# One query product a step earlier, value and probability products of self attention a step later, in a two-attention and experts kernel

## The chip, the cores and the metric

The kernel runs on one core of one Trainium2 chip. The metric is the device time of one execution, in microseconds, as the median of several runs. All times below that are not medians come from one profiled execution of the same program.

## The reference, cut to what matters

One layer with three residual parts over x of 32 batches, 32 positions and 256 features:

```python
x = x + xattn(layernorm(x), ctx_512, ...)   # 16 heads, 257 context rows of 64 features, rotary context
x = x + attn(layernorm(x), ...)             # self attention over the 32 positions of a batch, 16 heads of 128
x = x + ffn(layernorm(x), ...)              # router, 8 of 64 experts, capacity 128, silu gate

# self attention
q = x @ (wq_codes * repeat(wq_scales, 32)) + bq     # k and v in the same way
scores = einsum('bqhd,bkhd->bhqk', q, k) / sqrt(128)
out = einsum('bhqk,bkhd->bqhd', softmax(scores), v)
return out @ (wo_codes * repeat(wo_scales, 32)) + bo

# cross attention, after folding its weights
scores = einsum('bhsr,bhlr->bhsl', q_r, k_r)        # 257 keys a batch
ctx_c = einsum('bhsl,bld->bhsd', softmax(scores), kv_rope)
```

## The kernel before, in words

The 1024 rows of x are eight tiles of 128 rows, each holding four batches. A software pipeline of three stages runs over them: while tile i is in cross attention, tile i-1 is in self attention and tile i-2 in the output product of self attention and the router. Before the pipeline stands a part that folds and dequantises weights, behind it one that runs the 64 experts and adds their rows up. The change touches the pipeline alone.

A pipeline tile is 21 steps, written out by hand and the same on every engine. In step r (0 to 15) TensorE makes the scores of one row of cross attention (`score_row`, lines 1189 and 1190), VectorE takes the row's maximum (line 830), ScalarE the exponential (line 609). Two steps later TensorE transposes the probabilities (`transpose_row`, line 1197) and ScalarE copies them out of PSUM (line 617); three steps later TensorE sums them with the context (`sum_row`, line 1208). `score_row` waits for the exponential of two rows before, `transpose_row` for the copy of the transposes before, which have the same bank. After every four rows VectorE normalises one batch (`normalise`, lines 836 to 840), at the steps 6, 10, 14 and 18.

Around these steps lie *uses*: a use is a group of matmuls into one PSUM bank and the instructions on ScalarE and VectorE that drain it. Uses of cross attention alternate between banks 4 and 5 in the order of `XS`, those of self attention and router between banks 6 and 7 in the order of `SS`. A use waits until the one before it in its bank is drained. `X_AT` and `BEHIND` say in which step each use stands; on every engine the uses of `X_AT` come before those of `BEHIND` in one step. Every engine runs its instructions in the order written, and a wait holds up all that is behind it.

The names: `hT` is the transposed normalised input of a tile, `qa` and `qb` the two query products of cross attention for the next tile (line 1161; drained by two copies on ScalarE, line 588, then two subtractions on VectorE, line 824, that make the low halves), `kt0` to `kt3` the transposed contexts of the batches (line 1166; `kt0` is the next tile's), `cT0` to `cT3` transposes of the normalised results (line 1172), `out` the output product of cross attention (line 1176). In self attention `q0` to `k3` are query and key products, `sc` the scores (line 1235; its maximum and difference on VectorE, lines 872 and 873, its exponential on ScalarE, line 638), `v0` to `v3` the value products (lines 1142 to 1144 with 512 columns, six matmuls each; drained by ScalarE, line 630), `pv0` to `pv3` the products of values and probabilities (line 1245; drained by a copy on ScalarE, line 634, and a subtraction on VectorE, line 883), `wo0` to `wo3` the output product, whose result VectorE adds to x at step 4 of the next tile (line 928). `pos` is the router's count of places (lines 1259 and 1260). At step 15 VectorE computes the router's slots (`place`, lines 919 to 921), after which GpSimd scatters eight groups of rows (line 488). `cT3` waits for `normalise` of the last batch, `kt0` for the drain of `qb` (both in bank 4), `out` for the copy of `cT3`.

Tile 0 has no self attention beside it; tile 7 has no next tile, so its `qa`, `qb`, `hT` and `kt0` are skipped; then follow a pass with self attention alone (of tile 7) and one with only the output product of tile 7.

Of the kernel before, what the change touches and what calls it, by code (L numbers as in the profile page):

```python
# [31 lines left out]
XSPLIT = ["kt1", "kt2", "kt3", "qa", "qb", "kt0"]  # L32
XNEXT = ("hT", "qa", "qb", "kt0")

X_AT = {2: ["kt1"], 6: ["kt2"], 7: ["cT0"], 10: ["kt3"], 11: ["cT1"], 15: ["cT2", "hT"], 16: ["qa"], 18: ["qb"],
        19: ["cT3", "kt0"], 20: ["out"]}

SS = ["wo", "hT", "q0", "q1", "q2", "q3", "k0", "rT", "k1", "k2", "log", "k3", "sc", "v0", "pos", "v1", "v2", "v3",
      "pv0", "pv1", "pv2", "pv3"]
BEFORE = ("wo", "rT", "log", "pos")  # L40

BEHIND = {0: ["wo0"], 1: ["wo1"], 2: ["wo2"], 3: ["hT", "wo3"], 4: ["q0"], 5: ["q1"], 6: ["q2", "q3"], 7: ["k0", "rT"],
          8: ["k1", "k2", "log"], 9: ["k3"], 10: ["sc"], 11: ["v0", "pos"], 12: ["v1"], 13: ["v2"], 14: ["v3"],
          15: ["pv0"], 16: ["pv1"], 17: ["pv2"], 18: ["pv3"]}
WS = 16.0
STEPS = ROWS + 5

# [19 lines left out]
def build(nc, x, ctx_in, Wq, kcq, kckv, Wqr, Wkr, Wo_x, codes, scales, bq, bk, bv, bo, rw, gup, dnp,  # L67
# [5 lines left out]
    with ctx:  # L73
# [193 lines left out]
        def spos(name, j, more=1):  # L267
            name = name[:2] if name[:2] == "wo" else name
            n = SS.index(name)
            if name in BEFORE:  # L270
                j = j + 1
            return n % 2, j * (len(SS) // 2) + n // 2 + more

# [280 lines left out]
        def _(e):  # L554
# [44 lines left out]
            def exp_row(i, r):  # L599
                e.wait_ge(maxed, i * ROWS + r + 1)  # L600
                if r % RB == 0:

                    b = r // RB
                    if b >= 2:
                        e.wait_ge(on_ready, i * BT + b - 1)
                    elif not isinstance(i, int) or i > 0:
                        e.wait_ge(on_ready, i * BT + (b - 1))
                s = r % (2 * RB)
                e.activation(pr[:, s, :], bank[r % 2][:, 0:NL], ACT.Exp, bias=nmax[:, s:s + 1],  # L609
                             accum_out=rsum[:, s:s + 1]).then_inc(expd, 1)  # L610
# [39 lines left out]
            def tile(i, j, m, last=False):  # L650
# [8 lines left out]
                for r in range(STEPS):  # L659
                    if i is not None:  # L660
                        if 2 <= r <= ROWS + 1:
                            copy_row(i, r - 2)
                        if r < ROWS:
                            exp_row(i, r)
                        for name in X_AT.get(r, ()):
                            if name in XNEXT and not last:
# [43 lines left out]
        def _(e):  # L710
# [121 lines left out]
            def normalise(i, b):  # L832

                e.wait_ge(summed, i * ROWS + RB * (b + 1))
                e.wait_ge(last_ready, i * BT + b + 1)
                link(e.tensor_tensor(On[:, b % 2], bank[3][:, 0:RB * DC].rearrange("p (r d) -> p r d", r=RB),
                                     On[:, b % 2], ALU.add), "x", i)
                s = RB * (b % 2)
                link(e.reciprocal(rinv[:, s:s + RB], rsum[:, s:s + RB]), "x", i)
                e.tensor_tensor(On[:, b % 2], On[:, b % 2], rinv[:, s:s + RB].unsqueeze(2).to_broadcast([P, RB, DC]),  # L840
                                ALU.mult).then_inc(on_ready, 1)
# [108 lines left out]
            def tile(i, j, m, last=False):  # L950
# [9 lines left out]
                for r in range(STEPS):  # L960
                    if i is not None:
                        if r < ROWS:
                            max_row(i, r)
                        if r % RB == 2 and r > RB:
                            normalise(i, r // RB - 1)
                        for name in X_AT.get(r, ()):
                            if name in XSPLIT and name not in XNEXT:
# [95 lines left out]
        def _(e):  # L1063
# [136 lines left out]
            def sum_row(i, r):  # L1200
                b = r // RB
                e.wait_ge(pt_ready, i * ROWS + r + 1)
                if r % RB == 0:

                    e.wait_ge(on_ready, i * BT + b)
                o = DC * (r % RB)
                for c in range(2):
                    ins = e.matmul(bank[3][:, o:o + DC], pT[:, r % 2, c, :], Cr[:, b, c, 0, :], start=c == 0, stop=c == 1)  # L1208
                ins.then_inc(summed, 1)
# [82 lines left out]
            def tile(i, j, m, last=False):  # L1292
# [12 lines left out]
                for r in range(STEPS):  # L1305
                    if i is not None:
# [4 lines left out]
                        if 3 <= r <= ROWS + 2:  # L1311
                            sum_row(i, r - 3)
                        for name in X_AT.get(r, ()):
                            if name not in XNEXT:
# [101 lines left out]
```

## Time and profile before

| | us |
|---|---|
| median of 3 runs | 802.52 (801.3 to 803.19) |
| the profiled execution | 789.05 |
| its span in the profile | 787.2 |
| pipeline tiles 0 to 7 within it | about 80 to 557 |
| the two passes without cross attention | about 557 to 620 |
| experts and their sums | the rest |

In the rows further down a line of the merged timeline has the start, the duration (of all instructions that the line merges), engine, source line, operation, output and inputs, tile of the array, form, count, and in brackets the engine's idle time before it with what ended that.
### The profile page before, as it was taken

The page shows a single profiled execution, that of the slowest core. Times are in us where ns is not written, and L with a number is a line of the kernel's source. Part 1 is how long each engine was busy: PE and PEld are TensorE (multiplying, and loading weights), DVE is VectorE, ACT ScalarE, POOL GpSimd, SP SyncE. Part 2 cuts the span into 40 slices and gives each one's busy share as a digit, 9 for nine tenths or more (in the row PEclk, how much of TensorE's full clock was granted, in tenths as well). Part 3 has the DMA queues.
Part 4 walks back from the last instruction along what each step waited for, and adds up shares of the span by engine and source line. Part 5 has one row for each costly group of instructions (what it writes and reads, how often), then busy time and mean ns, then how long its engine had stood idle before and what let it go on. Part 6 is the DMA issues. An engine that isn't in the chain of part 4 may idle for free.

```text
span 787.2 us, 16249 instructions
## 1 busy us (share of the span) xinstructions
PE 646.7 (82%) x6211; PEld 525.5 (67%) x6211; DVE 426.1 (54%) x1091; ACT 288.8 (37%) x798; POOL 292.8 (37%) x279
## 2 busy tenths in 40 slices
PE   6976788999999998998999899899874178898850
PEld 4865467777868867776787687686754077777740
DVE  1274672654765764676576577467553223333334
ACT  1133563355354444336236336336031033333310
POOL 3125594213115314213312512300303337787780
PEclk9786557999999998999999999999998579999985
DMA  7986985995002002001100200100101069999988
GB/s 196 282 248 161 257 201 136 299 325 180 2 2 72 18 2 73 17 3 43 46 2 18 71 2 13 57 2 2 66 2 50 31 158 296 296 303 305 298 155 272
DMA packets 98987, 97.61 MB, mean 124 GB/s; under 512 B 26238, under 2 KB 92848, under 8 KB 98912
## 3 DMA queue, kind: packets, MB, share of 16 engines
q1 hardware_dynamic: 86016, 78.21, 34.3%
q0 software_dynamic: 12288, 17.95, 10.5%
q8 instruction: 51, 0.84, 0.4%
q10 hardware_dynamic: 608, 0.42, 0.2%
q14 instruction: 24, 0.20, 0.1%
HBM read 62.32 MB, written 35.19 MB: 124 GB/s over the span
## 4 chain that ended last, share of the span: by engine, by line
PE 51%; DVE 17%; issue 11%; DMA 7%; ACT 6%; POOL 6%; another core or an unknown queue 2%; SPq 0%; POOLq 0%; DVEq 0%; PEldq 0%; ACTq 0%
PE bank L1142 6%; PE bank L1144 5%; PE bank L1143 5%; POOL expert_sums L545 5%; PE bank L1176 5%; PE bank L1208 5%; DMA expert_sums<-Wh,etok 4%; PE bank L1161 4%; PE bank L1197 4%; PE bank L1245 3%; PE bank L1190 2%; PE bank L1131 1%; PE bank L1119 1%; DVE nmax L830 1%
## 5 line engine op out<-in xcount | busy, mean ns | idle before, releaser
L545 POOL DMA_INDIRECT expert_sums<-Wh,etok x64 | 98.9, 1545 | 38.8 <-issue 21.7
L488 POOL DMA_INDIRECT expert_rows<-h,slot x64 | 62.8, 981 | 87.9 <-DVE slot L921 70.9
L609 ACT ACTIVATE pr<-bank,nmax 128x257 f32<-128x257 f32 x128 | 61.2, 478 | 88.8 <-DVE nmax L830 87.5
L1142 PE MATMUL bank<-space,Wh 128*128 128x128 f16 x512 | 88.3, 219 | 5.8 <-DVE X L928 3.0
L1144 PE MATMUL bank<-space,Wl 128*128 128x128 f16 x512 | 88.2, 219 | 0.0
L1143 PE MATMUL bank<-space,Wh 128*128 128x128 f16 x512 | 88.1, 219 | 0.0
L471 POOL TENSOR_TENSOR Cr<-C,Ct 128x192 f32<-128x192 f32 x64 | 39.7, 645 | 116.6 <-PE bank L1208 116.4
L1208 PE MATMUL bank<-Cr,pT 128*128 128x64 f32 x512 | 77.9, 279 | 4.9 <-DVE On L840 4.5
L830 DVE TENSOR_REDUCE nmax<-bank 128x1 f32<-128x257 f32 x128 | 53.5, 419 | 47.5 <-PE bank L1190 45.3
L1208 PEld LDWEIGHTS bank<-Cr,pT 128*128 128x128 f32 x512 | 73.9, 208 | 6.6 <-issue 5.9
L479 POOL TENSOR_TENSOR On<-Cr,pr 128x256 f32<-128x256 f32 x32 | 20.7, 648 | 138.4 <-ACT pr L609 138.4
L617 ACT COPY pT<-bank 128x256 f32<-128x256 f32 x128 | 47.6, 372 | 65.2 <-PE bank L1197 64.1
L1346 PE MATMUL bank<-Wh,ring 128*96 128x128 f32 x512 | 68.1, 277 | 0.1
L867 DVE SCALAR_TENSOR_TENSOR space<-bank,bqk 128x512 f32<-128x512 f32 x64 | 43.6, 690 | 40.0 <-PE bank L1144 39.9
L1197 PE MATMUL bank<-ident,pr 128*128 128x128 f32 x256 | 58.9, 315 | 6.4 <-ACT pT L617 5.8
L1142 PE MATMUL bank<-Wh,space 128*128 128x256 f16 (+1 forms) x192 | 59.4, 309 | 4.5 <-ACT space L630 3.0
L1346 PEld LDWEIGHTS bank<-Wh,ring 128*96 128x96 f32 x512 | 60.9, 166 | 0.5 <-issue 0.4
L1144 PE MATMUL bank<-Wh,space 128*128 128x256 f16 (+1 forms) x192 | 59.1, 308 | 0.0
L1143 PE MATMUL bank<-Wl,space 128*128 128x256 f16 (+1 forms) x192 | 59.1, 308 | 0.0
L1142 PEld LDWEIGHTS bank<-space,Wh 128*128 128x128 f16 x512 | 51.2, 100 | 7.7 <-DVE X L928 4.3
L1355 PE MATMUL bank<-ring,Wh 96*128 96x256 f32 x128 | 43.0, 417 | 13.9 <-DVE Wh L1031 11.1
L1143 PEld LDWEIGHTS bank<-space,Wh 128*128 128x128 f16 x512 | 50.1, 98 | 0.1
(177 smaller groups left out, 1384.1 us busy)
## 6 DMA issues: line engine op xcount, KB each, us to landing
ring<-L_ffn_gate_up_proj_dram SPq DMA_DIRECT2D x64, 192.0 KB
expert_rows<-h SPq DMA_DIRECT2D x8, 1284.0 KB, 17.6
Wh<-expert_rows SPq DMA_DIRECT2D x64, 160.5 KB
ring<-L_ffn_down_proj_dram SPq DMA_DIRECT2D x64, 96.0 KB
expert_sums<-h SPq DMA_DIRECT2D x4, 1152.0 KB, 13.7
C<-ctx_dram SPq DMA_DIRECT2D x24, 128.0 KB, 4.0
Wl<-expert_sums SPq DMA_DIRECT2D x3, 1024.0 KB, 7.5
space<-L_xattn_Wo_dram SPq DMA_DIRECT2D x8, 256.0 KB, 5.0
```

The costliest lines, as they stand in the source:

```text
L488: e.indirect_dma_start(XE[:, :], bass.IndirectOffsetOnAxis(ap=slot[:, k:k + 1], axis=0), h3[:, :], None, bounds_check=E * CAP - 1, oob_is_ ...
L545: e.indirect_dma_start(Y[n % NY][:, :], bass.IndirectOffsetOnAxis(ap=etok[:, n % 4:n % 4 + 1], axis=0), ye[:, n % 4], None, bounds_check=Y ...
L609: e.activation(pr[:, s, :], bank[r % 2][:, 0:NL], ACT.Exp, bias=nmax[:, s:s + 1], accum_out=rsum[:, s:s + 1]).then_inc(expd, 1)
L617: e.copy(pT[:, r % 2], bank[2][:, 0:2 * P].rearrange("p (c t) -> p c t", c=2)).then_inc(pt_ready, 1)
L830: e.tensor_reduce(nmax[:, s:s + 1], bank[r % 2][:, 0:NL], AX.X, ALU.max, negate=True).then_inc(maxed, 1)
L867: e.scalar_tensor_tensor((qS, kS)[w][:, 4 * g:4 * g + 4, :], src[:, :].rearrange("p (h t) -> p h t", h=4), 1.0 / WS, bqk[:, w, 4 * g:4 * g ...
L1142: e.matmul(dst, ah, bh, start=first and n == 0, stop=False)
L1143: e.matmul(dst, ah, bl, start=False, stop=False)
L1144: ins = e.matmul(dst, al, bh, start=False, stop=last and n == len(terms) - 1)
L1197: ins = e.transpose(bank[2][:, c * P:(c + 1) * P], pr[:, r % (2 * RB), c * P:(c + 1) * P], ident[:, :])
L1208: ins = e.matmul(bank[3][:, o:o + DC], pT[:, r % 2, c, :], Cr[:, b, c, 0, :], start=c == 0, stop=c == 1)
L1346: ins = e.matmul(bank[2 + n % 2][0:I, half * P:(half + 1) * P], gu[:, n, c, half * I:(half + 1) * I], xeT[:, n % 2, c, :], start=c == 0, s ...
```

## The change

`qb` moves from step 18 to step 17. The uses `v0` to `v3` move from steps 11, 12, 13, 14 to 12, 13, 14, 15, and `pv0` to `pv3` from 15, 16, 17, 18 to 16, 17, 18, 19. `pos` stays at step 11, but since it now stands ahead of `v0` in the order of self attention, it and `v0` change banks.

```diff
-X_AT = {2: ["kt1"], 6: ["kt2"], 7: ["cT0"], 10: ["kt3"], 11: ["cT1"], 15: ["cT2", "hT"], 16: ["qa"], 18: ["qb"],
+X_AT = {2: ["kt1"], 6: ["kt2"], 7: ["cT0"], 10: ["kt3"], 11: ["cT1"], 15: ["cT2", "hT"], 16: ["qa"], 17: ["qb"],
         19: ["cT3", "kt0"], 20: ["out"]}
-          8: ["k1", "k2", "log"], 9: ["k3"], 10: ["sc"], 11: ["v0", "pos"], 12: ["v1"], 13: ["v2"], 14: ["v3"],
-          15: ["pv0"], 16: ["pv1"], 17: ["pv2"], 18: ["pv3"]}
+          8: ["k1", "k2", "log"], 9: ["k3"], 10: ["sc"], 11: ["pos"], 12: ["v0"], 13: ["v1"], 14: ["v2"],
+          15: ["v3"], 16: ["pv0"], 17: ["pv1"], 18: ["pv2"], 19: ["pv3"]}
```

VectorE at the end of a pipeline tile, before, from the last row's maximum (line 830) on. Lines 919 to 921 are the router's slots, 824 the low halves of `qa` (bank 5) and `qb` (bank 4), 836 to 840 the last batch's `normalise`, 883 the drains of `pv0` to `pv3`:

```order
L830 TENSOR_REDUCE nmax<-bank1 128x1
L883 TENSOR_TENSOR space<-bank6,space 128x512
L919 TENSOR_TENSOR space<-space,sv2 128x512
L920 TENSOR_REDUCE slotf<-space 128x8
L921 TENSOR_SCALAR slot<-slotf 128x8
L824 TENSOR_TENSOR qspace<-bank5,qspace 64x4x4x32 x2
L883 TENSOR_TENSOR space<-bank7,space 128x512
L883 TENSOR_TENSOR space<-bank6,space 128x512
L836 TENSOR_TENSOR On<-bank3,On 128x256
L839 RECIPROCAL rinv<-rsum 128x4
L840 TENSOR_TENSOR On<-On,rinv 128x256
L824 TENSOR_TENSOR qspace<-bank4,qspace 64x4x4x32 x2
```

The same place after, from the slots on:

```order
L919 TENSOR_TENSOR space<-space,sv2 128x512
L920 TENSOR_REDUCE slotf<-space 128x8
L921 TENSOR_SCALAR slot<-slotf 128x8
L824 TENSOR_TENSOR qspace<-bank5,qspace 64x4x4x32 x2
L883 TENSOR_TENSOR space<-bank6,space 128x512
L824 TENSOR_TENSOR qspace<-bank4,qspace 64x4x4x32 x2
L883 TENSOR_TENSOR space<-bank7,space 128x512
L836 TENSOR_TENSOR On<-bank3,On 128x256
L839 RECIPROCAL rinv<-rsum 128x4
L840 TENSOR_TENSOR On<-On,rinv 128x256
L883 TENSOR_TENSOR space<-bank6,space 128x512
```

The last `normalise` stood ahead of the low halves of `qb` and now stands behind them; the slots stood behind the drain of `pv0` and now stand ahead of it.

TensorE at the same place, before: line 1161 is `qa` (bank 5) and `qb` (bank 4), 1245 `pv1` (bank 7), `pv2` (bank 6) and `pv3` (bank 7), 1172 `cT3`, 1166 and 1167 `kt0`:

```order
L1161 MATMUL bank5<-h1T,M 128x128 x8
L1245 MATMUL bank7<-diag,space 128x128 x4
L1197 MATMUL bank2<-ident,pr 128x128 x2
L1208 MATMUL bank3<-Cr,pT 128x64 x2
L1245 MATMUL bank6<-diag,space 128x128 x4
L1208 MATMUL bank3<-Cr,pT 128x64 x2
L1161 MATMUL bank4<-h1T,M 128x128 x8
L1245 MATMUL bank7<-diag,space 128x128 x4
L1172 MATMUL bank5<-ident,On 128x128 x2
L1166 MATMUL bank4<-ident,Cr 128x128 x2
L1167 MATMUL bank4<-ident,Cr 128x1
L1176 MATMUL bank5<-N,cT 128x256 x8
```

After, from the transposes behind `qa` and `pv0` on:

```order
L1197 MATMUL bank2<-ident,pr 128x128 x2
L1208 MATMUL bank3<-Cr,pT 128x64 x2
L1161 MATMUL bank4<-h1T,M 128x128 x8
L1245 MATMUL bank7<-diag,space 128x128 x4
L1208 MATMUL bank3<-Cr,pT 128x64 x2
L1245 MATMUL bank6<-diag,space 128x128 x4
L1172 MATMUL bank5<-ident,On 128x128 x2
L1166 MATMUL bank4<-ident,Cr 128x128 x2
L1167 MATMUL bank4<-ident,Cr 128x1
L1245 MATMUL bank7<-diag,space 128x128 x4
L1176 MATMUL bank5<-N,cT 128x256 x8
```

Between `qb` and `cT3` there stood one group of line 1245; now two of them and a sum stand there, and the last group has moved between `kt0` and `out`.

TensorE in the middle of a tile, steps 11 and 12, after (line 1259 and 1260 are `pos`, 1189 and 1190 the scores of row 12, 1197 and 1208 transposes and sum, 1142 to 1144 `v0`):

```order
L1172 MATMUL bank4<-ident,On 128x128 x2
L1259 MATMUL bank7<-mask,before 128x64
L1260 MATMUL bank7<-count,ones16 128x64
L1189 MATMUL bank0<-KTh,qspace 128x257
L1190 MATMUL bank0<-KTl,qspace 128x257
L1197 MATMUL bank2<-ident,pr 128x128 x2
L1208 MATMUL bank3<-Cr,pT 128x64 x2
L1142 MATMUL bank6<-Wh,space 128x512
```

Before, the six matmuls of `v0` stood between line 1172 and line 1259, and those of `v1` behind line 1208.

## Rows read from the trace of the kernel before

**Rows 1.** Waits of TensorE from 125 to 560 us: waiter, releaser, total, times, longest:

```profile
PE bank L1166 <- DVE qspace L824: 7.3, 4, 2.4
PE bank L1166 <- issue: 7.2, 3, 2.4
...
PE bank L1172 <- DVE On L840: 1.0, 1, 1.0
```

**Rows 2.** Merged timeline, end of tile 2, all engines (columns as told above):

```profile
243.82 0.56 PE L1208 MATMUL bank<-Cr,pT 128*128 128x64 f32 x4
...
244.20 1.29 DVE L883 TENSOR_TENSOR space<-bank,space 128x512 f16<-128x512 f32 x2
244.22 2.00 PE L1161 MATMUL bank<-h1T,M 128*128 128x128 f32 x16
...
246.06 1.06 PE L1245 MATMUL bank<-diag,space 128*128 128x128 f32 x8
246.07 0.42 DVE L840 TENSOR_TENSOR On<-On,rinv 128x256 f32<-128x256 f32 x1
246.26 1.17 ACT L588 CAST qspace<-bank 64x512 f16<-64x512 f32 x2 [1.65 <-issue]
246.95 0.38 PE L1172 MATMUL bank<-ident,On 128*128 128x128 f32 x2
...
247.46 1.39 DVE L824 TENSOR_TENSOR qspace<-bank,qspace 64x512 f16<-64x512 f32 x2 [0.97 <-ACT qspace L588]
...
248.91 0.44 PE L1166 MATMUL bank<-ident,Cr 128*128 128x128 f32 x2 [1.58 <-DVE qspace L824]
...
249.43 3.72 PE L1176 MATMUL bank<-N,cT 128*128 128x256 f32 x16
```

**Rows 3.** Merged timeline, ends of tiles 0, 3 and 6:

```profile
131.08 5.41 PE L1176 MATMUL bank<-N,cT 128*128 128x256 f32 x16
...
306.35 1.17 ACT L588 CAST qspace<-bank 64x512 f16<-64x512 f32 x2 [2.44 <-PE bank L1161]
...
310.19 6.61 PE L1176 MATMUL bank<-N,cT 128*128 128x256 f32 x16 [0.53 <-ACT cT L597]
...
497.19 5.28 PE L1176 MATMUL bank<-N,cT 128*128 128x256 f32 x16 [0.63 <-ACT cT L597]
```

**Rows 4.** A stretch by windows: busy of PE, PEld, DVE, ACT, POOL, then granted clock, DMA:

```profile
312.00:315.00 3.00, 3.00 (x8) 2.36 (x7) 0.00 (x0) 0.00 (x0) 1.23 (x3) 0.50 0.32 95
```

**Rows 5.** Merged timeline, steps 11 and 12 of tile 4:

```profile
350.51 0.38 PE L1142 MATMUL bank<-Wh,space 128*128 128x512 f16 x1
...
351.43 0.63 ACT L638 ACTIVATE space<-space 128x512 f32<-128x512 f32 x1 [1.89 <-DVEq L875]
...
351.81 0.19 PE L1259 MATMUL bank<-mask,before 128*128 128x64 bf16 x1
...
351.96 0.35 ACT L617 COPY pT<-bank 128x256 f32<-128x256 f32 x1
...
352.71 0.56 PE L1208 MATMUL bank<-Cr,pT 128*128 128x64 f32 x4
...
353.60 0.39 PE L1142 MATMUL bank<-Wh,space 128*128 128x512 f16 x1 [0.34 <-ACT space L630]
```

**Rows 6.** Merged timeline, the pass with self attention alone:

```profile
585.20 0.15 DVE L915 TENSOR_SCALAR h<-h 128x1 f32<-128x1 f32 x1
...
593.34 1.41 DVE L883 TENSOR_TENSOR space<-bank,space 128x512 f16<-128x512 f32 x2
...
594.08 1.16 PE L1245 MATMUL bank<-diag,space 128*128 128x128 f32 x8 [0.68 <-DVE space L883]
...
601.64 0.27 PE L1142 MATMUL bank<-Wh,space 128*128 128x256 f16 x1
...
603.24 0.98 POOL L488 DMA_INDIRECT expert_rows<-h,slot  x1 [0.30 <-issue]
605.72 0.42 DVE L928 SCALAR_TENSOR_TENSOR X<-bank,X 128x256 f32<-128x256 f32 x1 [9.14 <-remote]
```

More of the change, by code:

```diff
@@ L33 @@
 XNEXT = ("hT", "qa", "qb", "kt0")
-X_AT = {2: ["kt1"], 6: ["kt2"], 7: ["cT0"], 10: ["kt3"], 11: ["cT1"], 15: ["cT2", "hT"], 16: ["qa"], 18: ["qb"],
+X_AT = {2: ["kt1"], 6: ["kt2"], 7: ["cT0"], 10: ["kt3"], 11: ["cT1"], 15: ["cT2", "hT"], 16: ["qa"], 17: ["qb"],
         19: ["cT3", "kt0"], 20: ["out"]}
-SS = ["wo", "hT", "q0", "q1", "q2", "q3", "k0", "rT", "k1", "k2", "log", "k3", "sc", "v0", "pos", "v1", "v2", "v3",
+SS = ["wo", "hT", "q0", "q1", "q2", "q3", "k0", "rT", "k1", "k2", "log", "k3", "sc", "pos", "v0", "v1", "v2", "v3",
       "pv0", "pv1", "pv2", "pv3"]
```

## The prediction

> **What bounds the kernel now.** I began with who waits for whom on TensorE within the pipeline, since the change moves uses of TensorE between steps. The longest item is line 1166, the transposes `kt0` at the end of a tile: 7.3 us in four waits and 7.2 in three, together 14.5 us in seven waits, one at the end of each of the tiles 0 to 6 [rows 1]. All else is short, so between these places TensorE sets the pace. Then I read the end of one tile. `kt0` starts at 248.91 after 1.58 us of idle, released by VectorE's low halves of `qb` (247.46, 1.39 long), which in turn followed ScalarE's copies at 246.26 [rows 2]. From the end of `qb` on TensorE (246.06, where `pv3` starts) to the start of `out` at 249.43 it takes 3.37 us [rows 2]. From tile 3 on that chain is longer. ScalarE idles 2.44 us before the copies of `qb` at 306.35, not 1.65 as in tile 2, so they start 0.8 us later after the matmuls, and `out` follows at 310.19, 3.84 after the copies' start in place of 3.17 (246.26 to 249.43): 3.37 + 0.8 + 0.67 = 4.84 us from the end of `qb` [rows 2, 3]. No row says why that hop is late.
>
> **The clock** is the second thing to see at these ends. The 16 records of `out` take 3.72 us at the end of tile 2 [rows 2], but 5.41, 6.61 and 5.28 at the ends of tiles 0, 3 and 6 [rows 3]; one of about the same size lies between (tile 4). The granted clock there is 0.50, the 1.2 GHz level, while TensorE is busy all the time [rows 4]; before it fell TensorE had stood idle for `kt0` and shortly for `out`. So these four cost 1.7, 2.9, about 1.7 and 1.6, in all 7.8 us.
>
> **Part 1, the end of a tile.** No instruction is added or removed. With the change `qb` is followed on TensorE by `pv1`, a sum and `pv2` before `cT3`: 0.89 (246.06 to 246.95), 0.40 (243.82 to 244.22) and 0.89, so 2.18 us of cover that the drain of `qb` did not have before [rows 2]. That is the gain. But VectorE goes through its list in order, and the last `normalise`, for which `cT3` waits, now stands behind the low halves of `qb` and the drain of `pv1`. From the end of `qb`: low halves start 1.40 later (as 247.46 against 246.06), last 1.39, drain of `pv1` 0.65 (half of 1.29), `normalise` 1.05 (it ends at 246.49, 1.0 behind the end of the two drains of line 883 at 245.49, and starts a little before that end), hop 0.1: `cT3` starts at 4.6 [rows 2]. TensorE is ready at 2.18, so it waits 2.4 us there, with `cT3` late next in place of `kt0`. Then 0.22 for `cT3`, 0.52 for `kt0` (248.91 to 249.43), 0.89 for `pv3`, which now stands there: `out` starts at 6.23 [rows 2]. `out` itself then finds the copy of `cT3` done, hidden by `kt0` and `pv3`. Since two products and a sum moved behind `qb`, its end comes 2.18 sooner. Net: 6.23 - 2.18 - 3.37 = +0.7 us for an end like that of tile 2; tile 1 has the same form, so +1.4 for two. In an end like tile 3's the chain grows by the same late hop (0.8), and before it took 4.84: 6.23 + 0.8 - 2.18 - 4.84 = 0.0 [rows 3]. The late hop could vanish with the other order (-0.8 each) or the tile could behave as tile 2 does (+0.7 each); I take 0 for the four tiles 3 to 6. Tile 0 has no `pv`: 4.6 - 0.65 + 0.74 for `cT3` and `kt0`, less 0.40 for the sum, less 3.36 now gives up to +0.9; I take half, +0.5, an estimate, as the sum ahead of `qb` there waits for a copy now. Tile 7 skips `qa` and `qb`; there `normalise` stood behind the drain of `pv2` and will stand ahead of it. Its `cT3` waits 1.0 us now [rows 1] and `out` about 0.6 behind it; one of the two can go, between 0 and 1.5 us; I take -0.9.
>
> **Part 2, the middle of a tile.** Here a cover is lost. ScalarE waits 1.89 us for the difference of the self-attention scores and only then runs their exponential (351.43), and behind it, in order, the copy of the transposed probabilities (351.96) [rows 5]. TensorE's next transposes and the sum at 352.71 need that copy, whatever TensorE did before. Today TensorE fills this time with `v0`, 350.51 to 351.81, 1.30 us [rows 5]. With `v0` one step later it stands idle instead. What comes back: `v1` now waits for the drain of `v0` in the same bank and starts at 353.60, while the sum at 352.71 needs only 0.40; in the changed order `v0` can start there, at 353.11, as the banks alternate: 0.49 back [rows 5]. Net 1.30 - 0.49 = +0.8 us a tile, and the next wait of TensorE lies at the tile's end, whose chain starts from `qb` and moves along, so nothing absorbs it. Seven tiles (1 to 7): +5.7. Bounds: 0 if the copy on line 617 comes as much sooner as `v0` is gone, 1.3 if `v0` also waits.
>
> **Part 3, the pass with self attention alone and the way to the experts.** The router's slots stood behind the drain of `pv0` and now follow line 915 at 585.20. They take 1.6 us and were ready at about 593.3 when line 883 went on [rows 6]; now at about 587, six us sooner. The drain of `pv1` no longer waits behind them, so `pv3`'s wait of 0.68 goes [rows 6]; one value copy more now stands in ScalarE's list ahead of `pv0`, about +0.3. Net -0.4. Larger is what follows: GpSimd's last issue of the scatter is at 603.24 (0.98 long), and VectorE's line 928 starts at 605.72 after 9.14 us, released by something that the profile does not name [rows 6]. The output product in front of it issues its last matmuls at 601.64 and just after [rows 6], so it is through by about 602.1. I take the 3.5 us between as belonging to the scatter, which ends at just that time; it would be over by 598 with the change: -3.5. Bounds: 0 and -3.6.
>
> **The clock again.** Each of seven ends keeps one wait of 2.4 us or more. Two, tiles 1 and 2, waited 1.58 us and kept full clock [rows 2]; with 2.4 they are near tile 0's, which lost it. One fall more than now, less luck: +1.5 us, an estimate, bounds -7.8 and +5.9.
>
> [...]
>
> **Sum.** 5.7 + 1.4 + 0 + 0.5 - 0.9 - 0.4 - 3.5 + 1.5 = +4.3 us on the profiled execution's 789.05 (span 787.2), so 793.4. The median of the runs lies 13.5 us above that execution; no row tells where, so I carry it unchanged: 802.52 + 4.3 = **806.8 us**.
>
> **The rivals.** (a) The gap before line 928 has another cause and stays: +3.5, 810.3. For it: the matmuls' late hops at tile ends are unexplained as well. (b) All seven ends lose the clock: 7 x 1.95 (the mean of the four) is 13.7 against 7.8, +5.9 in place of 1.5, 811.2. (c) Faster: the falls at the ends go. The waits at an end that lost the clock came in two pieces, 2.4 and 0.53 to 0.63 [rows 1, 3]; now the second is covered by `pv3` and TensorE works for 2.2 us between `qb` and the wait. If three or more of the four falls go, the clock term is -6 or below and the time 799.3. Against it: tile 0 fell after a wait of 2.4 with none before `out`. (d) The change does what its place suggests: `kt0` waits no more and nothing waits instead, -14.5 in place of the +1.9 at the ends makes the sum -12.1, 790.4. VectorE's order excludes it unless `normalise` is not the last thing `cT3` waits for. (e) Part 2's loss is absorbed: -5.7, 801.1, no change.
>
> **How the numbers follow.** Forecast 0.38, (a) 0.20, (b) 0.15, (c) 0.15, (d) 0.05, (e) 0.07. A measurement of this kernel can tell 0.2%, 1.6 us, from no change. (c) and (d) and a little of (e) are faster, 0.22; most of (e) and the low edge of the forecast are within, 0.13; the rest slower, 0.65. The range from (c) to beyond (b), 799.0 to 812.5, leaves out (d) and the two rivals (a) and (b) coming together (814.7); the terms' own bounds lie within it.
>
> **What the changed profile would show.** TensorE's long waits should be for `cT3` (line 1172, released by line 840), 2.4 us or more in tiles 1 to 6, and none for `kt0`. In the middle TensorE should wait over 1 us for line 617 ahead of line 1197 and no more for line 630. The scatter in the last pass should start near 588, and line 928 follow the output product at once. If line 1172 waits under 1 us, part 1 is wrong; if line 1197 does not wait, part 2; if line 928 still stands 3 us behind the matmuls, part 3.

## The result and the profile after

The changed kernel takes 830.9 us (median of 4 runs, 828.14 to 838.74), the kernel before beside it 801.9 us (794.85 to 803.19). The ratio is 1.047 with a 95% interval of 1.040 to 1.053: slower, by 29 us between the medians. Here and below a ratio compares only the executions in the faster of two states that these programs show, a median all of them, so the two can differ (4.7% of 802 us would be 37). The prediction had 806.8 us and a range up to 812.5. The sign was right, the size was wrong by a factor of seven.

The profiled execution of the changed kernel took 831.06 us (span 829.1, mean granted clock 0.878, before 787.2 and 0.902). Of the 42 us between the two spans, about 10 lie ahead of the first score, in code that the change doesn't touch; this part varies from one execution to the next (last section). So I compare the tiles, from the start of one output product (`out`, line 1176) to the next. Before, the seven distances from tile 0 to tile 7 were 60.0, 58.4, 60.8, 63.6, 63.5, 59.9 and 56.2 us (249.43, 310.19, 497.19 of [rows 2, 3] are three of the starts). After, they are 60.6, 63.1, 71.4, 66.5, 67.2, 67.6 and 57.3: together 31 us more, nearly all of it in the tiles that have a scatter. The stretch from the `out` of tile 1 to that of tile 7 holds 30.6 of them (kernel before, then changed kernel; the columns are length, busy time of PE, PEld, DVE, ACT and POOL, the granted clock, and the DMA engines' share and GB/s):

```profile
191.04:553.39 362.35, 335.52 (x3756) 271.16 (x3756) 236.42 (x609) 161.46 (x469) 99.16 (x122) 0.98 0.08 25
203.55:596.51 392.96, 347.62 (x3758) 280.20 (x3756) 233.69 (x607) 163.11 (x468) 102.69 (x126) 0.93 0.07 24
```

TensorE does the same work in both. It stands idle for 26.8 us in the first and 45.3 in the second, and is busy for 12.1 us longer, as the clock is at 0.50 for 58.0 us of the second and 13.7 of the first. So two fifths of the loss are the clock's.

TensorE's waits in the pipeline of the changed kernel, 125 to 610 us (waiter, releaser, total, times, longest), to be read beside [rows 1]:

```profile
PE bank L1172 <- DVE On L840: 34.3, 7, 6.9
PE bank L1197 <- ACT pT L617: 12.3, 9, 3.3
...
PE bank L1176 <- ACT cT L597: 1.0, 2, 0.8
```

The wait for `kt0` is gone and the wait for `cT3` (line 1172) has taken its place, as foreseen. But it is 34.3 us long, where about 15 were expected. The mid-tile wait for line 617 is new too, also as foreseen. The end of tile 4 in the merged timeline shows what is in the long wait (two cuts of it):

```profile
386.81 0.40 DVE L921 TENSOR_SCALAR slot<-slotf 128x8 uint32<-128x8 f32 x1
...
388.09 1.01 POOL L488 DMA_INDIRECT expert_rows<-h,slot  x1 [0.90 <-DVE slot L921]
...
389.50 1.17 ACT L588 CAST qspace<-bank 64x512 f16<-64x512 f32 x2 [1.59 <-PE bank L1161]
...
390.81 2.00 PE L1161 MATMUL bank<-h1T,M 128*128 128x128 f32 x16
...
395.35 1.17 ACT L588 CAST qspace<-bank 64x512 f16<-64x512 f32 x2 [3.79 <-remote]
...
397.07 0.97 POOL L488 DMA_INDIRECT expert_rows<-h,slot  x1 [0.30 <-issue]
398.27 0.59 ACT L634 CAST space<-bank 128x512 f16<-128x512 f32 x1 [1.75 <-remote]
...
399.80 0.59 ACT L634 CAST space<-bank 128x512 f16<-128x512 f32 x1 [0.95 <-remote]
...
400.38 0.85 DVE L840 TENSOR_TENSOR On<-On,rinv 128x256 f32<-128x256 f32 x1
...
401.38 0.66 PE L1172 MATMUL bank<-ident,On 128*128 128x128 f32 x2 [6.33 <-DVE On L840]
```

The product `qb` issues its matmuls from 390.81 on and is through at about 392.8. ScalarE has nothing else to do, and yet it starts the copies at 395.35, some 2.5 us later, where the copies of `qa` at 389.50 came promptly behind their product. The two copies of line 634 behind it are late as well. The normalise (lines 836 to 840) waits for the drain between them and for the last of the tile's sums (line 1208), and `cT3` for the normalise. All three late starts carry the mark "remote": a semaphore moved just before, but no instruction ended then. The trace's record of semaphore updates shows what they waited for: the signal of `qb`, due at 392.81, arrives at 395.32; those of `pv1` and `pv2`, due at 393.70 and 395.04, at 398.24 and 399.78; that of the sum, due at 394.10, at 399.68. All were due while GpSimd issued the eight parts of its scatter (line 488), from 388.09 to 398.04, and the last arrives 1.7 us behind its end. Before the change this scatter began 1.4 us ahead of `qb` (366.17 against 367.56 in tile 4); now it begins 2.7 us ahead. In tile 1, which has no scatter, the same wait for `cT3` is 2.27 us, near the 2.4 of the prediction.

The granted clock follows (columns as above). [rows 4] showed one such stretch:

```profile
394.00:397.00 3.00, 1.04 (x9) 0.85 (x8) 0.45 (x1) 1.16 (x2) 2.16 (x3) 1.00 0.30 110
397.00:400.00 3.00, 0.00 (x0) 0.00 (x0) 1.91 (x4) 0.79 (x2) 1.16 (x2) 0.80 0.30 110
400.00:403.00 3.00, 1.62 (x7) 1.31 (x8) 1.76 (x4) 1.07 (x3) 0.94 (x2) 0.50 0.24 56
```

In the middle of a tile it falls too, which it did not before. Tile 2, at step 11, first the matmuls, then two windows:

```profile
241.53 0.46 PE L1197 MATMUL bank<-ident,pr 128*128 128x128 f32 x2 [1.40 <-ACT pT L617]
...
242.54 0.63 PE L1142 MATMUL bank<-Wh,space 128*128 128x512 f16 x1
```

```profile
238.00:241.00 3.00, 1.33 (x11) 0.93 (x10) 2.75 (x8) 1.12 (x4) 0.00 (x0) 1.00 0.00 0
241.00:244.00 3.00, 2.47 (x10) 1.64 (x11) 2.79 (x8) 1.97 (x8) 0.62 (x1) 0.63 0.00 0
244.00:247.00 3.00, 3.00 (x16) 1.46 (x14) 0.83 (x2) 1.56 (x5) 0.00 (x0) 0.80 0.00 0
```

The matmul of 512 columns takes 0.63 us there and 0.38 at full clock [rows 5]. Against full clock these last two windows lack 3 x 0.37 + 3 x 0.20 = 1.7 us, a little less in work, as TensorE was idle for 0.5 of them.

### The profile page after: what moved, and what is told of

The parts are those of the page before. It is cut to its first block, busy times and chain, and to the rows that moved or that the text cites. A ratio compares the mean times of both kernels' runs of the same rounds, so it can differ in the third digit from the quotient of the medians.

```text
span 829.1 us, 16248 instructions
## 1 busy us (share of the span) xinstructions
PE 668.9 (81%) x6211; PEld 542.4 (65%) x6211; DVE 421.3 (51%) x1091; ACT 291.1 (35%) x798; POOL 291.5 (35%) x279
## 4 chain that ended last, share of the span: by engine, by line
PE 53%; DVE 14%; issue 10%; DMA 7%; POOL 6%; ACT 4%; another core or an unknown queue 3%; SPq 1%; POOLq 0%; DVEq 0%; ACTq 0%; PEldq 0%
PE bank L1142 7%; PE bank L1144 7%; PE bank L1143 7%; POOL expert_sums L545 5%; PE bank L1176 5%; PE bank L1208 4%; PE bank L1197 4%; DMA expert_sums<-Wh,etok 4%; PE bank L1161 3%; PE bank L1190 2%; PE bank L1245 2%; ACT qspace L588 2%; PE bank L1131 2%; PE bank L1119 1%
## 5 line engine op out<-in xcount | busy, mean ns | idle before, releaser
L1142 PE MATMUL bank<-Wh,space 128*128 128x256 f16 (+1 forms) x192 | 62.2, 324 | 4.9 <-DVE space L883 2.6
L1143 PE MATMUL bank<-Wl,space 128*128 128x256 f16 (+1 forms) x192 | 62.0, 323 | 0.0
L1144 PE MATMUL bank<-Wh,space 128*128 128x256 f16 (+1 forms) x192 | 61.8, 322 | 0.0
L1142 PEld LDWEIGHTS bank<-space,Wh 128*128 128x128 f16 x512 | 51.2, 100 | 5.5 <-DVE X L928 2.1
L824 DVE TENSOR_TENSOR qspace<-bank,qspace 64x512 f16<-64x512 f32 x32 | 22.0, 689 | 58.1 <-ACT qspace L588 47.2
```

What stands on the lines that cost most here:

```text
L1142: e.matmul(dst, ah, bh, start=first and n == 0, stop=False)
L1143: e.matmul(dst, ah, bl, start=False, stop=False)
L1144: ins = e.matmul(dst, al, bh, start=False, stop=last and n == len(terms) - 1)
```

## Experiments

My theory (A in the expectations): the change moves the router's slots (`place`, lines 919 to 921) ahead of the drain of `pv0` in VectorE's list in every tile, so the scatter starts earlier against the chain that ends a tile, and signals come late while it runs. The rivals: the place of `qb` (C), the shift of the value products (D), VectorE's order of low halves and normalise (B), or late signals that have nothing to do with the scatter (E).

### The change in parts, and the slots alone

`qb` alone is the kernel before with this line:

```diff
-X_AT = {... 16: ["qa"], 18: ["qb"],
+X_AT = {... 16: ["qa"], 17: ["qb"],
```

> The kernel before with the product qb at step 17 and nothing else moved. The changed kernel is about 29 us (3.6%) above the one before; the mid-tile wait for line 617 explains 7 x 0.8 = 5.7 of them, and about 20 us lie at the tile ends. Theory A (the router's slots stand ahead of the drain of pv0 in VectorE's list, so GpSimd's scatter starts some 3 us earlier against the chain that ends a tile, and ScalarE and VectorE pick up their signals late while it runs): here the slots stay where they were, so the ends keep about the 2.4 us wait for cT3 that a tile without a scatter shows; the time is 800 to 810 us with the kernel before at 802. Theory C (it is qb's place, with normalise behind its low halves, whatever the scatter does): the waits for cT3 are 6 us in tiles 3 to 6 and the time is 820 to 828. Theory D (it is the shift of the value products and of pv0 to pv3): 800 to 804.

Measured: 798.3 us, 0.9986 of the kernel before beside it (0.993 to 1.004). No change; the range of 800 to 810 had taken the kernel before at 802, and it took 798.2 here. The wait of 2.27 us for `cT3` stands in place of that for `kt0`, and nothing grows. C falls.

The other part alone is the changed kernel with that line put back:

> The changed kernel with qb put back to step 18: the value products, pv0 to pv3 and with them the router's pos one step shifted, the slots ahead of the drain of pv0. Theory A: the scatter starts early here too, so the late hops at the ends stay in tiles 3 to 6: the mid-tile wait of 1.4 us (+5.7 us net) and 5 to 15 us at the ends, 812 to 822 us with the kernel before at 802. Theory C: only the mid-tile wait, 806 to 810. Theory D: nearly the whole, 825 to 832.

Measured: 826.5 us, 1.038 (1.027 to 1.049). Nearly the whole loss, more than I gave A. That alone doesn't tell A from D, since this part holds both the shift and the earlier slots. Its tile 4:

```profile
380.49 1.00 POOL L488 DMA_INDIRECT expert_rows<-h,slot  x1 [0.90 <-DVE slot L921]
...
384.67 2.00 PE L1161 MATMUL bank<-h1T,M 128*128 128x128 f32 x16
...
389.66 0.97 POOL L488 DMA_INDIRECT expert_rows<-h,slot  x1 [0.30 <-issue]
...
390.65 1.14 POOL L471 TENSOR_TENSOR Cr<-C,Ct 128x192 f32<-128x192 f32 x2
...
391.87 1.17 ACT L588 CAST qspace<-bank 64x512 f16<-64x512 f32 x2 [6.55 <-remote]
```

The scatter starts 4.2 us ahead of `qb` here, and the copies of `qb` start 5.2 us after their product is through, a little after the scatter's last issue (389.66, through at 390.63). In the record of semaphore updates, the signal of `qb` arrives at 391.84, that of `pv2` behind it at 391.94 and that of `cT3` at 391.98. TensorE issued the first two 1.84 us apart (384.67 and 386.51), and `cT3` 0.89 us later. Signals that arrive within 0.14 us of one another were held back together; it was not the work that came late.

The slots alone, undone in the changed kernel (first edit) and done in the kernel before (second edit):

```diff
-                    if m is not None and r == 15:
+                    if m is not None and r == 16:
                         place(m)
```

```diff
+                    if m is not None and r == 15:
+                        place(m)
                     uses(BEHIND.get(r, ()))
...
-                    if m is not None and r == 15:
-                        place(m)
```

> The changed kernel with one thing undone: VectorE computes the router's slots at step 16 behind the drain of pv0, as it stood before, so that the scatter starts about 3 us later than in the changed kernel. TensorE's and ScalarE's lists are those of the changed kernel. Theory A: the waits for cT3 in tiles 3 to 6 fall from 6 to 7 us towards the 2.3 us of tile 1, fewer falls of the clock follow, and the time is 808 to 818 us with the changed kernel at about 829. Theories C and D (the place of qb, or the shift, with VectorE's order of low halves and normalise): the time stays at 826 to 832, a few tenths more for the slots in the chain.

> The kernel before with one thing added: VectorE computes the router's slots at step 15 ahead of the drain of pv0, so that the scatter starts 1 to 3 us earlier; no other list changes. Theory A: the hops behind qb come late at more ends and the wait for kt0 in tiles 3 to 6 grows from 3.4 or less to 4 or more, time 806 to 818 us with the kernel before at 802. Theories C and D: 800 to 803, with the last pass's scatter a few us sooner at most.

Measured, beside a kernel before of 798.2 us: 807.2 us, 1.014 (1.003 to 1.025), for the first and 820.0 us, 1.027 (1.019 to 1.035), for the second; they lie 1 and 2 us outside the ranges that I gave A. Three small VectorE operations (1.6 us) put in another place of its list make the kernel before 22 us slower, and take over 20 us off the changed one (830.9 in the first group of runs). From the `out` of tile 1 to that of tile 7 the two traces take 368.4 and 383.3 us. D falls with it, as the first keeps the shift. In the second, the wait for `kt0` has grown from at most 2.4 us [rows 1] to 7:

```profile
PE bank L1166 <- DVE qspace L824: 29.3, 6, 7.0
PE bank L1208 <- DVE On L840: 4.5, 6, 0.8
PE bank L1166 <- issue: 4.3, 1, 4.3
```

### Without the scatter, and with a later one

In both kernels GpSimd waits for the slots and issues nothing in tiles 2 to 7:

```diff
                     if b == BT - 1 and m is not None:
-                        scatter(m)
+                        e.wait_ge(slot_ready, m + 1)
...
                 if m is not None:
-                    scattered(m)
+                    e.sem_inc(h3_free, 1)
```

> The kernel before without the scatter of rows to the experts in the six tiles 2 to 7 (GpSimd still waits for the slots; the two scatters behind the pipeline remain; the experts' stage then works on zero rows for these tiles). Theory A (late hops while the scatter runs): the end of every tile looks like that of tile 1, kt0 waits 1.4 to 1.6 us, 0.8 to 2 us are saved in tiles 3 to 6 with their falls of the clock, 786 to 794 us with the kernel before at 798. Rival E (the hops are late for a reason that the scatter only marks): 797 to 800.

> The changed kernel with the same left out. Theory A: the waits for cT3 are 2.2 to 2.6 us in every tile, and the change costs then what the prediction's parts 1 and 2 say, about 6 to 9 us against the kernel before without its scatter: 794 to 802 us. Rival E: 822 to 830 us, and the waits for cT3 stay at 6 us.

Measured beside a kernel before of 802.0 us: 782.8 us (0.981, 0.973 to 0.989; faster than A had it) and 795.5 us (0.992, 0.986 to 0.999). E falls: no copy is late in either trace. The row of the kernel before's variant, then that of the changed one's, 125 to 600 us:

```profile
PE bank L1166 <- DVE qspace L824: 11.7, 7, 2.2
```

```profile
PE bank L1172 <- DVE On L840: 18.3, 8, 3.5
PE bank L1197 <- ACT pT L617: 9.9, 8, 1.4
```

Every wait for `kt0` is 1.57 or 1.58 us from tile 1 on, and each wait for `cT3` from tile 1 to tile 6 is 2.27. By the medians the scatter costs the kernel before 19 us as well, and the changed one 35 (from 830.9); that is 16 of the 29 us, and the other 13 are the order itself. The ratios alone give the order 1.1%, some 9 us, with bounds of about 0 and 17. The traces settle it nearer to the medians. From the `out` of tile 1 to that of tile 7, the kernel before's variant, then the changed one's:

```profile
188.33:538.81 350.48, 332.02 (x3756) 268.60 (x3756) 232.10 (x609) 161.77 (x469) 57.34 (x79) 0.99 0.03 6
199.90:564.11 364.21, 337.58 (x3758) 272.94 (x3756) 232.37 (x607) 163.40 (x468) 57.42 (x79) 0.97 0.03 6
```

So of the 30.6 us between the two kernels in this stretch 13.7 are the order, and 16.9 the growth of what the scatter costs (11.9 before, 28.8 after). The order's 13.7 are 8.1 of idle time and 5.6 of work at a lower clock. The prediction's own waits, with its +0.7 at the ends of tiles 2 to 6 in place of 0, give 6 x 0.8 + 5 x 0.7 - 0.9 = 7.4 us of idle time here: the waits were right, the clock was not.

Then the scatter behind the chain, in the changed kernel and in the one before:

```diff
-                    if b == BT - 1 and m is not None:
-                        scatter(m)
                     if not last:
                         rope_sums(i + 1, b)
+                    if b == BT - 1 and m is not None:
+                        e.wait_ge(on_ready, i * BT + BT)
+                        scatter(m)
```

> The changed kernel with GpSimd's scatter put behind the rope sums of the next tile's last block and behind the last normalise of the tile (a wait for its result), so that it starts when the chain at the tile end is through. Theory A: as without the scatter there, cT3 waits 2.2 to 2.6 us, and the late hops move to the first steps of the next tile, where ScalarE's exponentials set TensorE's pace with 0.1 to 0.5 us to spare: 800 to 812 us against 829 of the changed kernel. Rival E: no change at the ends, 825 to 832.

> The kernel before with the scatter put behind its last normalise in the same way. Theory A: kt0 waits 1.4 to 1.6 us in every tile in place of up to 2.4 with a second wait behind it, three or four falls of the clock go, 788 to 796 us, if the first steps of the next tile take the 10 us of the scatter without loss; if they are slowed as the ends were, 798 to 806. Rival E: 797 to 800, with the waits for kt0 as in the kernel before.

Measured: 814.4 us, 1.021 (1.012 to 1.031), and 799.4 us, 0.996 (0.989 to 1.003). The first is 2 us above A's range; in the second the clause "if they are slowed as the ends were" came true. The ends are clean in both, and the late signals have moved to the first steps of the next tile. In tile 4's scatter of the first, the scores of the second step are through at 398.57, VectorE takes their maximum at 402.10, and the exponential at 402.56 follows 4.67 us of idle time on ScalarE. The scatter takes its toll there too; in the changed kernel the end of a tile is the dearer place (814.4 against 830.9), in the one before neither is (799.4 against 802.0).

### One chip without late signals

> The changed kernel with one thing moved on VectorE: the low halves of qb stand at step 18 behind the last normalise, not ahead of it. Theory A (signals come late while the scatter runs): in tiles 3 to 6 the normalise waits for the drain of pv1, whose data come late by themselves, so cT3 waits 5 us or more still and kt0 waits about 1.4 us behind it: 826 to 838 us. Rival B (VectorE's order makes the wait: normalise held up by 1.39 us of low halves): the wait for cT3 falls from 6 us to 4.5 or less with only 1 us given back at kt0, and falls of the clock go: 812 to 822 us.

> The changed kernel with the six scatters of the pipeline writing rows of 32 numbers (128 B) to another table in place of 321 (1284 B): GpSimd issues the same eight instructions with the same count of rows, a tenth of the bytes moves; the experts' rows of these tiles stay zero. If the late signals come from the bytes in flight (theory A1): cT3 waits 2.3 us, 795 to 803 us, as without the scatter. If they come from GpSimd's making of the descriptors or from their number (theory A2): cT3 waits about 6 us, 820 to 830 us.

> The changed kernel with each of the six scatters replaced by eight plain stores of the same 128 rows of 1284 B to a table of their own, issued by SyncE when the slots are ready; GpSimd does nothing for them, and the experts' rows of these tiles stay zero. The same 1.3 MB move at the same point of the tile, in a shorter time. Theory A1 (bytes in flight): signals are late there too, cT3 waits 3.5 us or more in tiles 3 to 6, 808 to 830 us. Theory A2 (GpSimd's making of the descriptors): cT3 waits 2.3 us, 794 to 803 us.

> The kernel before with the router's slots computed at step 17 behind the drain of pv2 in place of step 15, so that the scatter starts some 2.5 to 3 us later. Theory A: qb's signal is on time in tiles 3 to 6 too, kt0 waits 1.6 us there in place of 1.7 to 2.4, out waits no second time, and falls of the clock go: 788 to 797 us with the kernel before at 800; what the later scatter holds up instead at the next tile's start may take some of it back, up to 801. If the place of the scatter has nothing to do with it: 799 to 802.

These four ran on another chip, on which the kernel before took 777.6 us. Measured: 794.7 us, 1.016 (1.006 to 1.027); 801.8, 1.018 (1.001 to 1.035); 796.8, 1.022 (1.009 to 1.035); 793.3, 1.012 (1.005 to 1.019). As tests of what they were made for they are void: no signal of TensorE to ScalarE or VectorE is late in any of the four traces. The first one has the scatter of tile 4 3 us ahead of `qb`, as in the changed kernel above, and the copies of `qb` come promptly:

```profile
371.42 1.01 POOL L488 DMA_INDIRECT expert_rows<-h,slot  x1 [0.90 <-DVE slot L921]
...
374.37 2.00 PE L1165 MATMUL bank<-h1T,M 128*128 128x128 f32 x16
...
376.41 1.17 ACT L588 CAST qspace<-bank 64x512 f16<-64x512 f32 x2 [1.29 <-PE bank L1165]
```

And the kernel before, at 777.6 us, is about what it was elsewhere with the scatter left out (782.8). Nor do plain stores in place of the scatter save anything here that can be told (1.022 against 1.018 with the scatter of short rows), though in the one trace of each the stretch from tile 1's `out` to tile 7's is 10 us shorter with them, 363.0 against 373.3; what the scatter still costs without late signals stays open. So the late signals depend on something besides the program, in these runs on the chip or on what else set this group apart. The fourth run says in addition that a later scatter, its last passes included, costs 1.2% where there are no late signals to avoid.

### Bytes or descriptors

The first three again beside the changed kernel itself, on a further chip. The edits, in this order: rows of 128 B to another table; plain stores by SyncE, with nothing issued by GpSimd in these tiles; low halves of `qb` at step 18 behind the normalise.

```diff
-                    e.indirect_dma_start(XE[:, :], ..., h3[:, :], None,
+                    e.indirect_dma_start((XE if cols == ROW else SHORT)[:, :], ..., h3[:, 0:cols], None,
...
-                        scatter(m)
+                        scatter(m, 32)
```

```diff
+            def plain_rows(m):
+                e.wait_ge(slot_ready, m + 1)
+                for k in range(TOPK):
+                    e.dma_start(PL[P * k:P * k + P, :], h3[:, :]).then_inc(plain, 16)
```

```diff
                         for name in X_AT.get(r, ()):
+                            if name == "qb":
+                                continue
...
+                        if r == 18 and not last:
+                            x_low("qb", i + 1)
```

> The changed kernel unaltered, beside the kernel before on one more chip. If the chip is like the first two (the kernel before at 798 to 802 us), theory A says 826 to 834 us with late signals under the scatter in tiles 3 to 6. If it is like the last one (the kernel before near 778 us and no late signal), the change costs only what it cost without the scatter, 12 to 17 us, 790 to 795 us. A rival in which the changed order makes the late signals by itself says 3.5% or more over the kernel before on any chip.

> The changed kernel with the pipeline's scatters cut to rows of 128 B. On a chip that shows late signals in the changed kernel: theory A1 (bytes in flight) 793 to 803 us and waits for cT3 of 2.3 us; theory A2 (GpSimd's descriptors) 820 to 832 us and waits of 6 us. On a chip without them it tells nothing: within 0.5% of the changed kernel.

> The changed kernel with eight plain stores by SyncE in place of each scatter. On a chip that shows late signals in the changed kernel: theory A1 (bytes in flight) 808 to 832 us and waits for cT3 over 3.5 us; theory A2 (GpSimd's descriptors) 793 to 803 us and waits of 2.3 us. On a chip without them: within 0.5% of the changed kernel or a little below.

> The changed kernel with VectorE's low halves of qb behind the last normalise. Without late signals the wait for cT3 was 1.5 us or less and the one for kt0 about 0.9 in the last look; with them, theory A says that both data come late whatever their order, 822 to 838 us beside a changed kernel at 830. Rival B (VectorE's order makes most of the loss) says 812 or less. On a chip without late signals: equal to the changed kernel within 0.5%, as the two short waits add up to the one long wait.

Measured, with the kernel before at 795.8 us: the changed kernel 821.9 us, 1.027 (1.018 to 1.036), late signals in tiles 2 to 6 as in the first trace; short rows 827.7, 1.037 (1.031 to 1.043); plain stores 792.6, 0.999 (0.994 to 1.004); normalise first 828.0, 1.037 (1.029 to 1.044). TensorE's longest group of waits in these four, in this order (the lines are shifted by the edits; 1172, 1173, 1184 and 1176 are all `cT3`):

```profile
PE bank L1172 <- DVE On L840: 32.6, 7, 6.1
```

```profile
PE bank L1173 <- DVE On L841: 35.3, 8, 6.7
```

```profile
PE bank L1184 <- DVE On L852: 18.3, 8, 3.5
```

```profile
PE bank L1176 <- DVE On L840: 30.1, 7, 6.0
```

It is not the bytes. With a tenth of them the wait is as long; with all of them moved by SyncE's stores, at up to 364 GB/s and in about half the time, it is that of the kernel without a scatter. What holds the signals back goes with the indirect DMAs that GpSimd issues, and it costs 29 us between the medians (821.9 to 792.6) on this chip, 2.8% by the ratios. Whether it is the issuing, the descriptors or their completion no run separates. B falls too: with the low halves behind the normalise the wait stays at 6 us, since ScalarE's copies are late by themselves.

The Trainium skill, DMA: Bandwidth & Descriptors (section "SWDGE vs HWDGE vs iDMA"), says that a DMA issued from GpSimd has its descriptors written by software into rings in the on-chip memory, and one issued from SyncE does not: hardware makes its descriptors. The two runs, short rows and plain stores, differ along this line, though also in being indirect or not. Why signals are held back on some chips only, no run here shows.

### The last passes, and a version that beats both

The slots ahead of the drain of `pv0` in the two passes behind the pipeline alone (second), and with it step 17 in the pipeline (first):

```diff
+                    if m is not None and i is None and r == 15:
+                        place(m)
                     uses(BEHIND.get(r, ()))
...
-                    if m is not None and r == 15:
+                    if m is not None and i is not None and r == 17:
```

> The kernel before with the router's slots at step 17 behind the drain of pv2 in the pipeline's tiles (scatter 2 to 3 us later there) and ahead of the drain of pv0 in the two passes behind the pipeline. On a chip with late signals (the kernel before near 796 to 802 us): theory A says that qb's signal is on time in tiles 3 to 6, fewer falls of the clock, and the last passes gain as in g2: 784 to 794 us. If the later scatter holds up the next tile's start as much: 793 to 799. On a chip without late signals: within 0.5% of the kernel before.

> The kernel before with the router's slots ahead of the drain of pv0 in the two passes behind the pipeline alone. Part 3 of the prediction says -3.9 us, as TensorE's wait for the normalised rows (line 811, which waits for the scatter's end) was 8.2 us before and 4.7 in the changed kernel; from the tail behind the last tile's out, which was 1.2 us shorter in the changed kernel, -1 us.

Measured on one more chip (kernel before 796.1 us): 788.3 us, 0.993 (0.989 to 0.997), and 794.0 us, 0.993 (0.988 to 0.998), by the ratio -5.5 us with bounds of -1.4 and -9.5. Both are faster than either kernel, by 0.7% of the one before. The second agrees with part 3's -3.9. Whether the later scatter in the pipeline adds anything stays open: by the ratios it doesn't, by the medians it adds 5.7 us. The copies of `qb` are prompt in the first one's trace, and the row maxima of the next tile's first steps up to 1.7 us late, as with the scatter behind the chain.

## Why the prediction was wrong, step by step

**What failed** is one sentence of part 1: "In an end like tile 3's the chain grows by the same late hop (0.8)", and from it "I take 0 for the four tiles 3 to 6". I had seen the late hop, had said that no row tells why, and then carried it as a constant into a changed order. It was no constant. It depended on where the scatter stood, and the change moves the scatter. Part 3 had this very fact, that the slots come earlier once they no longer stand behind the drain of `pv0`, but counted it only where it helped, in the last pass. In the pipeline the drain and the slots stand in the same order. The term was 0; the growth of the scatter's toll measured 16 us by the medians and 16.9 in the traces. There were also more late hops than the one that I had carried: in tile 4 of the kernel before, the signals of `pv3` and `cT3`, due at 370.45 and 370.67, arrive at 371.87 and 373.29.

**Part 1 otherwise** held. The wait for `cT3` was to be 2.4 us; it is 2.27 in tile 1, which has no scatter, and in every tile once the scatter is left out, against 1.57 for `kt0`: +0.7 each. With that, the ends of tiles 3 to 6 had to cost +0.7 each too, not 0, wherever the scatter is out of the way. `qb` alone changes nothing that can be measured.

**Part 2** held in its mechanism and wait (1.40 us ahead of line 1197 where about 1.3 were predicted, and none for line 630). The clock on top of it was missed. The text gave the clock a term for the ends only; the new wait in the middle of the tile brings falls of its own, 1.7 us in tile 2. With the scatter left out, the pipeline of the changed kernel still has six stretches at the lower clock behind tile 0, that of the kernel before two, and they cost it 5.6 us more of busy time, where the sum had 1.5 for the clock. The rest of the gap between the 13 us measured without the scatter and the 4.3 predicted is mostly the four ends just named (2.8).

**Part 3** held in what it foresaw: TensorE's wait for line 811, which follows line 928, fell from 8.2 to 4.7 us, and line 928 now follows TensorE's output product, not something unnamed:

```profile
648.14 0.42 DVE L928 SCALAR_TENSOR_TENSOR X<-bank,X 128x256 f32<-128x256 f32 x1 [7.25 <-PE bank L1144]
```

Before, it stood 9.14 us with the mark "remote" [rows 6], until after the scatter's end. It was a held signal as well (due at about 602.1, arrived at 605.70), and the first place where I could have read the mechanism: part 3 said that the gap belongs to the scatter, but took the scatter for what line 928 waits for, where no such wait is in the code. In the changed kernel a part of the gain is lost again, as TensorE waits 2.6 us for line 883 there (1.5 before); the tail behind tile 7's `out` is only 1.2 us shorter, where 3.9 were predicted.

**The clock term** of +1.5 us, with a bound of +5.9, was too small for the same reason. In the changed kernel the clock falls at the ends of tiles 2 to 6, where TensorE waits 3 to 6.9 us, and with the falls in mid-tile the busy time grows by 12.1 us. Rival (b) named this, but for waits of 2.4 us. The text also passed over an end that spoke against its reading: tile 5 of the kernel before waited 2.42 us for `kt0` and 0.63 for `out`, as tiles 3 and 6 did, and kept full clock (its `out` at 437.30 took 3.69 us). Of the other rivals, (a) fell with the gap before line 928, (c) since the falls grew in number, (d) as VectorE's order said it would, and (e) since nothing absorbed the wait in the middle. The case that came, a scatter that reaches into the chain, was not among them.

## What to carry to other kernels

The long idle times marked "remote" in this kernel were not noise: before carrying one over as a constant, ask what runs beside it each time it appears and whether the change moves that. Operations that cost nothing themselves can still decide when another engine starts something long; follow the whole chain, here from VectorE's slots to GpSimd's scatter. And weigh an effect in every place where the edit makes it, not only where it helps.

## What the hardware showed that I had not expected

While GpSimd issues its eight indirect DMAs (10 us), signals of TensorE reach ScalarE and VectorE late in every group of runs but one, and in that one, on its chip, none does. The longest delay was 5.7 us (a `pv` product in tile 3 of the changed kernel), and signals still arrived up to 1.7 us behind the last issue. None that was due within 3.3 us of the first issue was late by more than 0.25 us (`qb` alone: scatter at 381.49, signal due at 383.5, on time; changed kernel: scatter at 388.09, signal due at 392.8, late); some that were due later came promptly too. What lies beneath stays open.

The same program reached its first `out` at 131 to 132 us in some executions and at 137 to 145 in most (plain stores: 131.4 on one chip, 138.4 on another), and in these two the granted clock was at 0.50 for 75.1 and 93.5 us of the time before it. In two others it doesn't tell them apart (82.1 us before a first `out` at 132.0, 83.3 before one at 140.0). This is why single executions of this kernel can't be compared end to end.
